# Graph network on one core: where count products, block emptying and a tile's first one-hots stand in the first layer's order

## What is computed

```python
h = node_feat @ W_emb + b_emb
norm = _edge_norm(etype, dst, h.dtype)
for l in range(L):                                   # L = 2
    W = jnp.einsum('rb,bdf->rdf', w_coe[l], bases[l])
    T = jnp.einsum('nd,rdf->rnf', h, W)
    msg = T[etype, src] * norm
    agg = jax.ops.segment_sum(msg, dst, num_segments=N)
    h = agg + h @ self_loop[l]
    h = bn_gamma[l] * (h - bn_mean[l]) * jax.lax.rsqrt(bn_var[l] + BN_EPS) + bn_beta[l]
    h = jax.nn.relu(h)
```

## Time and profile before

| | |
|---|---|
| three runs | 6645.26, 6646.34, 6676.93 us; median 6646.34 |
| the profiled execution | 6596.08 us, its span 6594.3 us |
| first layer stage | 237.4 to 3681.1 us of the span |
| TensorE matmuls / weight loads | 69% / 52% of the span |
| VectorE, ScalarE, GpSimd | 58%, 37%, 37% |

### The profile page before, as it was taken

The page is one execution under the profiler, slowest core; times in us unless marked ns, Lnnn a source line. Parts: engine busy times, 40 slices in busy tenths (PEclk is TensorE's granted clock), DMA queues, the critical chain, the costliest instruction groups (busy, mean ns, idle before and its releaser), DMA issues. The chain is left out here.

```text
span 6594.3 us, 158005 instructions
## 1 busy us (share of the span) xinstructions
PE 4572.3 (69%) x54120; PEld 3419.2 (52%) x54121; DVE 3830.4 (58%) x8449; ACT 2466.9 (37%) x3932; POOL 2432.9 (37%) x2046
## 2 busy tenths in 40 slices
PE   5465556556666666666666499999989566666879
PEld 2244444444444444444444366666655366666868
DVE  4155555555555555555555566666640699999942
ACT  2122323223323323323323366666620355555700
POOL 0444444444454444454444000000000077776700
PEclk9777777777777777787777699999999778888889
DMA  5444444444444444444444422222259333344378
GB/s 199 139 126 138 139 137 142 136 136 138 139 138 138 140 135 137 141 139 137 139 137 142 146 77 80 77 79 77 78 189 299 111 142 145 148 156 150 113 234 282
DMA packets 678649, 935.70 MB, mean 142 GB/s; under 512 B 150867, under 2 KB 573374, under 8 KB 672542
## 3 DMA queue, kind: packets, MB, share of 16 engines
q1 hardware_dynamic: 469222, 545.66, 26.1%
q10 hardware_dynamic: 152888, 273.31, 11.3%
q0 software_dynamic: 56448, 115.72, 7.0%
HBM read 653.23 MB, written 281.17 MB: 142 GB/s over the span
## 5 line engine op out<-in xcount | busy, mean ns | idle before, releaser
L643 POOL DMA_INDIRECT f_rows<-table,f_recs x1715 | 1654.0, 964 | 1902.3 <-DMA f_recs<-edge_records 1187.8
L756 PE MATMUL f_acc<-f_rows,f_hot 128*128 128x264 f32 x3430 | 1214.2, 521 | 366.7 <-issue 285.1
L756 PEld LDWEIGHTS f_acc<-f_rows,f_hot 128*128 128x128 f32 x3430 | 868.8, 263 | 573.2 <-issue 348.4
L2067 PE MATMUL a_psum<-state_and_spare,a_weights 128*128 (+1 forms) x4802 | 664.3, 309 | 303.6 <-DVE a_weights L2200 168.9
L2017 POOL TENSOR_TENSOR a_weights<-a_powers,a_counts 128x896 f32<-128x896 f16 x245 | 713.6, 2917 | 315.9 <-ACT a_powers L2107 285.6
L2067 PEld LDWEIGHTS a_psum<-state_and_spare,a_weights 128*128 128x128 f32 x4802 | 653.7, 225 | 317.2 <-issue 215.0
L1224 ACT ACTIVATE g_grow<-g_gps 128x512 f16<-128x512 f32 x1225 | 667.1, 595 | 343.1 <-PE g_gps L1161 343.1
L816 ACT ACTIVATE f_counts_by_destination<-f_pm 128x896 f16<-128x896 f16 x343 | 314.5, 917 | 1011.5 <-PE f_pm L723 836.3
L705 PE MATMUL f_cnt<-f_dhot,state_and_spare 32*128 32x32 f16 x9604 | 239.2, 182 | 614.2 <-issue 614.1
L1181 PE MATMUL g_zps<-g_ohot,g_grow 32*128 32x256 f16 x19992 | 655.7, 269 | 0.0
L1263 DVE TENSOR_SCALAR g_ohot<-count,slot_target 128x256 f16<-128x256 f16 x2499 | 537.2, 282 | 152.4 <-PE g_zps L1181 147.0
(11 more groups left out here) (280 smaller groups left out, 6006.6 us busy)
## 6 DMA issues: line engine op xcount, KB each, us to landing
f_rows<-in_edge_attr SPq DMA_DIRECT2D x343, 320.0 KB
g_srow<-slot_sources SPq DMA_DIRECT2D x245, 320.0 KB
counts_by_destination_f<-f_counts_by_destination ACTq DMA_DIRECT2D x343, 224.0 KB
no_edge_penalty<-f_pen ACTq DMA_DIRECT2D x343, 224.0 KB
s_ring<-counts_by_destination_f SPq DMA_DIRECT2D x98, 784.0 KB
a_pen<-no_edge_penalty SPq DMA_DIRECT2D x49, 1568.0 KB, 10.0
a_counts<-counts_by_source_f SPq DMA_DIRECT2D x49, 1568.0 KB, 6.8
e_ring<-counts_by_source_f SPq DMA_DIRECT2D x343, 224.0 KB, 3.7
```

Source lines behind the costliest of these rows:

```text
L643: e.indirect_dma_start(out=rows[:, j, 0:D], out_offset=None, in_=k.table_d[0], in_offset=bass.IndirectOffsetOnAxis(ap=recs[:, j, 4:5].bitc ...
L756: m = e.matmul(acc[:, 0:GW], hot[:, j, :], rows[:, j, :], start=j == 0, stop=j == SLOTS - 1)
L2067: m = e.matmul(psum[:, 4 + i // 3, i % 3 * (D + 4):i % 3 * (D + 4) + D + 1], weights[:, j, i * P:(i + 1) * P], k.msg[:, bass.ds(hb * SEG + ...
```

## The change

Three things are moved; no product, copy or transfer is added or left out.

- TensorE, tiles of the loop: the 8 products of `begin_count(t - 1, b)`, with its two waits, are issued after the first sum of group b + 2, and the block's 64 small products in four parts of 16 behind the second to the fifth sum of that group. `ring` is raised at the fifth sum, before the last part. The last tile's counts, after the loop, stay as they were.
- ScalarE: block b is emptied before `move_turned(t, b - 1)`.
- VectorE: `tile_rows` and the one-hots of group 0 of tile t + 1 are made at the end of tile t, behind `rows_of_slots(t)`, and so ahead of `take(t)` and `hits(t + 1)`; the last tile is written out after the loop.

```diff
-            def count(t, b):
+            def begin_count(t, b):
...
-                for j in range(n):
+            def count_cells(b, first_cell, end_cell):
+
+                lo, n = BLOCKS[b]
+                for j in range(first_cell, end_cell):
...
-                    for j in range(g * PER, (g + 1) * PER):
+                    b = g - 2
+                    between = 0 <= b < len(BLOCKS) and not first
+                    for i in range(PER):
+                        j = g * PER + i
                         m = e.matmul(acc[:, 0:GW], hot[:, j, :], rows[:, j, :], start=j == 0, stop=j == SLOTS - 1)
-                    m.then_inc(ring, 1)
+                        if i == PER - 1:
+                            m.then_inc(ring, 1)
+                        if between and i == 0:
+                            begin_count(t - 1, b)
+                        n = BLOCKS[b][1] if between and i else 0
+                        part = range((i - 1) * n // (PER - 1), i * n // (PER - 1))
+                        if len(part):
+                            c = count_cells(b, part.start, part.stop)
+                            if part.stop == n:
+                                c.then_inc(counted, 1)
...
-                        if 2 <= g < 2 + len(BLOCKS):
-                            count(t - 1, g - 2)
...
                 for b, (lo, n) in enumerate(BLOCKS):
-                    if b:
-                        move_turned(t, b - 1)
                     e.wait_ge(counted, t * len(BLOCKS) + (b + 3))
...
                                 mine[:, lo:lo + n, :].rearrange("p j d -> p (j d)")).then_inc(stored, 16)
+                    if b:
+                        move_turned(t, b - 1)
...
-            def tile(t, first):
+
+            def tile(t, first, final):
                 if not first:
                     take(t - 1)
                 hits(t)
                 for g in range(GROUPS):
...
+                    if g:
+                        one_hots(t, g)
...
                 rows_of_slots(t)
+                if not final:
+                    own_rows(t + 1)
+                    one_hots(t + 1, 0)
+
+            own_rows(0)
+            one_hots(0, 0)
+            tile(0, True, False)
+            with e.Fori(1, NT - 1) as t:
+                tile(t, False, False)
+            tile(NT - 1, False, True)
```

More of the change, by code:

```diff
@@ L706, in count @@
                                      start=False, stop=j == n - 1)
-                m.then_inc(counted, 1)
+                return m
+            def count(t, b):
+                begin_count(t, b)
+                count_cells(b, 0, BLOCKS[b][1]).then_inc(counted, 1)
             def turn_counts(t, g, final=False):
@@ L877, in _, with own_rows, one_hots @@
             quads = lambda ap: ap.rearrange("p (u c) -> p u c", c=QCOLS)
+            def own_rows(t):
+                e.tensor_scalar(tile_rows, count_up[:, 0:P], k.tbase[:, bass.ds(t, 1)], None, ALU.subtract)
+                e.drain()
+            def one_hots(t, g):
+                e.wait_ge(rec_in[g], (t + 1) * 16)
+                e.wait_ge(ring, t * GROUPS + (g + 1))
+                s = slice(g * PER, (g + 1) * PER)
+                e.tensor_tensor(hot[:, s, :], repeat(tile_rows, PER), spread(recs[:, s, 0], P), ALU.is_equal)
+                e.tensor_tensor(rows[:, s, 2 * D:], repeat(k.iota8[:, :], PER),
+                                spread(recs[:, s, 3], RELATIONS), ALU.is_equal).then_inc(hot_made, 1)
             def hits(t):
-                e.tensor_scalar(tile_rows, count_up[:, 0:P], k.tbase[:, bass.ds(t, 1)], None, ALU.subtract)
                 e.wait_ge(wrec_in, (t + 1) * (16 * QUARTERS))
@@ L1040, in tile @@
                 rows_of_slots(t)
-            tile(0, True)
-            with e.Fori(1, NT) as t:
-                tile(t, False)
+                if not final:
[7 more added lines that the diff above has]
+            tile(NT - 1, False, True)
             take(NT - 1)
```

## The result

The kernel after takes 6697.4 us (median of 16 runs, 6677.26 to 6718.1), the kernel before 6661.97 us on the same chips (16 runs, 6633.6 to 6699.02). The ratio is 1.0055, 95% interval 1.0037 to 1.0074: slower by 35 us, 0.74 us a tile of the loop. The profiled execution took 6693.33 us; that of before, 6596.08, was faster than all its other runs, so the two traces differ by 97 us. I read from them what changed. Their gap is 62 us wider than that of the medians, so no difference between these two traces gives the size of the loss; sizes come from the medians.

What follows compares the result with a forecast made beforehand. TensorE, short of products while GpSimd issues gathers, was taken as the bound. Terms of -0.5 (group 0's one-hots), -0.2 (block 2's tie) and +0.5 (product changes) gave -0.2 us a tile, -10 us: 6636 us, no change; range 6380 to 6800.

Steps and rivals of the forecast that it cites:

- the side I gave 30% together: The sign slower: 29% for a rival at 6785 us and 1% from the forecast's own range.
- Changes between small and whole products: TensorE's 9 more returns a tile from 32-row products to a sum: +0.5 us a tile, ends 0 and 1.6.
- The new wait ahead of block 1: In group 3 TensorE idles 4.9 us until ScalarE has emptied block 0's banks; ends 0.36 and 4.9.
- Block 0 in group 2: The fifth sum stalls until group 1's gathers end, so the run parts and group 3 starts 3.7 us sooner; ends 0, -5.9.
- Block 2, the tie: In group 4, fifth sum held until group 3's gathers end, -2.5 us a tile, or out before, +2.1; taken -0.2.
- one run becomes two: Faster rival: group 4's fifth sum stays in and group 0 starts sooner, -3.3 us a tile, 6486 us; 26%.
- The long run stays: Slower rival: group 4's fifth sum gets out before group 3's gathers end, +2.9 us a tile, 6785 us; 29%.
- Group 0's one-hots: Made at the tile's end, sums start 4.3 us earlier but placing products stall: -0.5 us a tile, ends 0 and -6.5.
- ScalarE's order: Block 1 emptied three us sooner takes away the wait ahead of block 2, but the stall behind hides it: 0.
- The end of the stage: The counts after the loop keep their order; no term in the sum.
- The rule of the supply: While GpSimd issues gathers, TensorE gets 50 to 65 products, then about one a us until 2 to 2.7 us after.
- The cure's rival: Faster rival: parts of 16 among sums pass under gathers, the 614 and 51 us of issue time go, 6221 us; 14%.

Runs made afterwards that it cites:

- with the wait gone: The changed kernel, with ScalarE also emptying block 0 ahead of the last turned piece of the tile before: 6474.29 us, 0.9813 of the kernel before.
- late release: Kernel before, with only the ring release of groups 2 to 4 put off to the last but one product of the block behind: 6521.06 against 6622.79 us.

## Why the prediction was wrong

The forecast was -0.2 us a tile, 6636 us, no change. Measured is +0.74 us a tile, beyond 0.5%, on the side I gave 30% together. The time lies in my range, but by luck: the near miss hides large errors that cancelled.

**The step that failed is the last of the sum, "Changes between small and whole products", +0.5 us a tile with ends 0 and 1.6.** TensorE's busy time rose by 5.0 us a tile (4.1 with the wait gone, 5.0 in the kernels with plain reads, 239 / 48; there the spread costs 6.0 us of time a tile, 286 / 48). I counted 9 returns to a sum. There are 13: 4 in each of three blocks, since the 8 products of `begin_count` also stand between two sums, and one in block 3. And I bounded a change by the small product's own length, 0.18 us, on the return only, though there are two changes for each: 26 more at 0.15 us are 3.9 us. The rest of the 5.0 I put down to the longer stay at the half clock, by the mean clocks alone (0.74 against 0.77 here, 0.89 against 0.93 with plain reads). I also put most of it in the stalls. How much of it the stalls hide no run shows: with them the spread, its wait gone, still gained 53 us, by less idle time. No row of before has a sum beside a small product; the rule of the page was the only warning, and I had passed it over.

**The new wait ahead of block 1** was foretold at 4.9 us and is 4.70, at its place and for its reason. Its price was undersized: I let group 4 start 1.3 us later on its account. Taking it away gained 4.1 us a tile. I named "may bring the half clock" only in a rival, where the earlier trace rows already showed a group at 0.52 after idle time. It belonged in the sum.

**Block 0 in group 2** went as predicted: group 2's gathers stand apart. **Block 2, the tie,** fell on the fast side in this tile: the second half of the fifth sum came at 2117.66, 1.2 us after the end of group 3's gathers, and group 4's begin 4.62 us after that end. That is the mechanism of the rival "one run becomes two". L705's issue time fell to 263 where I wrote that it would stay above 400, and all idle time fell by 2.9 us a tile. The 6486 us didn't come: that rival's sum (-2.5 and -0.8) held nothing for the changes and nothing for the half clock behind the wait. "The long run stays" had the sign for a reason that didn't hold: the runs did part.

**Group 0's one-hots** at the tile's end: the sums start 0.6 us after the copy where the next tile isn't held by a turn (2129.30 against 2128.69) and take 2.46 us, the full clock, and the placing products stall instead, both as written. I took -0.5; by itself the part gains 65 us, 1.35 a tile. **ScalarE's order** I set at 0; alone it gains 112 us, 2.3 a tile. The first lies inside its ends, for the second I had given none; both were credited too little. What they shorten is shown on the chip without stalls (above). With stalls I have only L705's issue time, 479.0 us for the one-hots and 484.0 for ScalarE's order against 614.1, while that of the placing products grew from 51.5 to 236.8 and 98.5. **The end of the stage** kept its order.

**The rule of the supply** (50 to 65 products, then about one a us until the run ends) held in kind on the chips that show it. That the gathers cause it is now shown (plain reads take it away), and that moving the gathers cures part of it (late release, -102 us). The cure's rival, that parts of 16 pass, is refuted: the parts stall singly at 2114.81 and 2116.23. So is my reason for it. The Trainium skill, TensorE: Matmul & The Clock Gate (Architectural detail: the array is 16x 32x32), gives TensorE a queue of 64 instructions. From that I had worked out that a part of 16 products with its 16 loads passes, and it stalled after 14 and 15 products; the page doesn't say how fast the queue is filled.

What stays open: how the gathers keep work from TensorE; why one chip doesn't show it; how much of the +35 us is spread over the single causes on a chip with stalls, as parts don't add up there. The changed kernel was not run on the chip without stalls. The best version was not tried with fewer changes, say each block in two parts.

## What to carry to other kernels

Where an engine's idle time is to be filled by interleaving, compare its busy time before and after, not only its idle time: with the wait gone, 274 us less idle came with 196 us more busy, and without the stalls 286 us were lost. Small-tile and whole-array products should stay in long pieces, about 0.15 us a change here, and a wait put in among products can cost the half clock behind it as well as its length: the one of 4.7 us did, the one of 1.26 us didn't. To keep two engines' phases apart, move the semaphore that starts the other one before you move products: on a chip with stalls a release put off by some products gained 72 us where the spread, without its wait, gained 53.

## What the runs showed of the chip

- While GpSimd issues indirect gathers, one each 1.25 us, TensorE gets about one product a us once the first 50 to 65 are through; with plain reads of the same bytes the kernel takes 5630 in place of 6609 us and no small product has idle time of the kind "issue".
- One of the four chips of the experiments runs the same kernel, gathers and all, in 5649 us, 15% faster than the others, and shows no such stall. So a time of this kernel is compared with one of the same chip.
- A change between whole and 32-row products costs about 0.15 us at the full clock (1.21 us for 8), and the weight loads stand idle for 0.35 us under a sum that small products follow.
- Behind 4.7 us of idle time the granted clock was 0.52, and a sum among small products took 1.25 us in place of 0.71. Behind 1.26 us of idle time it stayed at 0.71.
